# A fused attention and mixture kernel: FFN matmuls in runs of ten at even steps, attention sums in runs of four at odd steps

## The chip, the cores and the metric

One Trainium2 chip, 8 cores, one program on all of them. Each core takes 1024 of the 8192 tokens (half a sequence of 2048) and reads the other half of its sequence for the keys; no core talks to another. The metric is the device time in microseconds of the slowest core. The engines are named as the profile names them: PE (TensorE), PEld (its weight loads), DVE (VectorE), ACT (ScalarE), POOL (GpSimd), SP (SyncE).

## What is computed

```python
xn = layernorm(x)                                   # x: 4 x 2048 x 4096
C_q, C_kv = xn @ Wq_d + bq_d, xn @ Wkv_d + bkv_d    # 12 and 4 columns
q = (C_q @ W_qk + b_qk) as 32 heads of 4
attn = softmax(q @ C_kv.T / 2)                      # per head, 2048 keys
s = (attn @ (C_kv @ Wv_u + bv_u)) @ Wo + bo         # heads of 128
base = xn @ base_W.T                                # 4096 x 4096
top 2 of 28 experts by xn @ gate_W.T, softmax of the two
lora = sum over experts of gate * 2 * (xn @ lora_A.T) @ lora_B.T
x = x + s * silu(base + lora)
```

## The kernel before

The layout is transposed: features on the 128 partitions, the core's T = 1024 tokens along the free axis, in two chunks of 512 (NCH = 2), so nearly every step is a pair of matmuls with 512 columns of tokens each. It runs in three stages.

First, statistics of both halves of the sequence, the normalised input xnT (32 blocks of 128 features, bf16, kept in SBUF), the latents cq_b (12 rows), ckv_b (4 rows x 2048 keys), and the gated LoRA activations hg1 and hg2.

Second, the head loop, `for h in range(H)` with H = 32, in which head h of the attention and output block h of the base and LoRA product (the FFN block) are computed together. It has SKT = 16 steps `kt`, one for each block of 128 keys. The matmuls of a head on PE, 138 in all:

- FFN (L846): 68 matmuls into the PSUM region FC, 64 with xnT against the weight block bw_bf and 4 with hg. `emit_ffn(n)` issues the next n of them. Before, kt 0 to 13 issue five each (four at kt 12 and 13).
- scores (L868): one pair for each kt, 4 rows (the latent dimension) by 128 keys, into one of two PSUM pairs, PB[kt % 2]. ACT reads the pair and writes exp into one of the four slots of pbuf (L971).
- a2 (L706): `a2block(t, h, j)` multiplies the exp of key block j with kaug (8 columns: ones and the latent keys) and accumulates over j in the PSUM region A2C, which is one for all heads. It is issued three steps late: at kt 3 the block 0 of head h, and at kt 0, 1 and 2 of the next head the blocks 13, 14 and 15.
- q of the next head (L878) after the scores of kt 6, bcd (L749, the reciprocal of the softmax sum spread over 128 rows) after those of kt 8, and up (L759, the heads' values) after those of kt 10: a pair each, into the PSUM pair that the next scores, those of kt 7, 9 and 11, are to use.

The waits that matter are these. The first a2 block of head h waits, chunk by chunk, for `("a2s", h-1, c)`: DVE copying the finished sums of head h-1 out of A2C (L904), which itself waits for block 15. The scores of kt wait for exp of kt-2, and those of kt 7, 9 and 11 wait, chunk by chunk, for DVE to have emptied the pair: `("qev", ...)` (L911), `("dcp", ...)` (L770) and `("uptt", ...)` (L776). Exp of kt waits for a2 of kt-4 (pbuf has four slots). `W(eng, *keys)` puts such waits on an engine; each engine works through its list in order. ACT also makes the reciprocal of the sum (L978, L981) behind exp 5. The FFN block of head h is scaled by DVE (L919) into fsb and stored by POOL, and the next FFN block waits for that. The weight block of head h+2 is loaded by POOL when the last FFN matmul of head h is done.

Third, the output projection (L1041), 2048 matmuls, with silu, product and residual on ACT and DVE.

Behind the last head stand a2 blocks 13 to 15, bcd and up of head 31 alone.

Of the kernel before, what the change touches and what calls it, by code (L numbers as in the profile page):

```python
# [20 lines left out]
def build(cfg):  # L21
# [3 lines left out]
    SKT = (2 * T) // 128  # L25
# [46 lines left out]
    with es:  # L72
# [64 lines left out]
        def I(instr, sem, key=None, n=1):  # L137
            cnt[sem] += n
            instr.then_inc(sems[sem], n)
            if key is not None:  # L140
                reg(key, sem)
            return instr
# [6 lines left out]
        def W(eng, *keys):  # L149
            best = {}  # L150
            for k in keys:
                if k is None or k not in EV:
                    continue
                s, v = EV[k]
                if v > 0:
                    best[s] = max(best.get(s, 0), v)
            for s, v in best.items():
                eng.wait_ge(sems[s], v)

        def vself(v):  # L160
            if cnt["sV"] > 0:
                v.wait_ge(sems["sV"], cnt["sV"])
# [532 lines left out]
        def a2block(t, hh, j, explicit_exp=False):  # L695
            if explicit_exp:
                W(t, ("exp", hh, j))
            u = hh * SKT + j
            mm = None
            for c, (c0, cw) in enumerate(CH):  # L700
                if j == 0:
                    if hh > 0:
                        W(t, ("a2s", hh - 1, c))
                    elif c == 0:
                        W(t, ("ckev1",), ("kgo",))
                mm = t.matmul(arena[0:8, A2C + c0:A2C + c0 + cw],  # L706
                              kaug[:, 8 * j:8 * j + 8],
                              pbuf[:, (u % NPB) * T + c0:(u % NPB) * T + c0 + cw],
                              start=(j == 0), stop=(j == SKT - 1),
                              skip_group_check=True)  # L710
            I(mm, "sT", ("a2", hh, j))
# [95 lines left out]
        for h in range(H):  # L807
            base_s = cnt["sS"]
            for kt in range(SKT):
                extra = 2 if (kt > DKT and h > 0) else 0  # L810
                EV[("exp", h, kt)] = ("sS", base_s + kt + 1 + extra)
            base_s += SKT + (2 if h > 0 else 0)
            cnt["sS"] = base_s
            if h == H - 1:
                EV[("dinv", h)] = ("sS", base_s + 2)
            else:
                EV[("dinv", h)] = ("sS", base_s + DKT + 3)
            off = cnt["sV"]
            if h > 0:
                for c in range(NCH):  # L820
                    EV[("a2s", h - 1, c)] = ("sV", off + c + 1)
                off += NCH
            if h + 1 < H:
                for ci in range(NCH):
                    EV[("qev", h + 1, ci)] = ("sV", off + ci + 1)
                off += NCH
            if h > 0:
                for qc in range(NCH):
                    EV[("dcp", h - 1, qc)] = ("sV", off + qc + 1)
                off += NCH  # L830
                for qc in range(NCH):
                    EV[("uptt", h - 1, qc)] = ("sV", off + qc + 1)
                off += NCH
            EV[("fcp", h)] = ("sV", off + 1)

            @block.tensor
            def _(t, h=h):
                fq = list(ffn_mms(h))
                fpos = [0]

                def emit_ffn(n):
                    while n > 0 and fpos[0] < len(fq):
                        lhsT, rhs, c0, cw, st_, sp_ = fq[fpos[0]]
                        if fpos[0] == 0:
                            W(t, ("wLb", h), ("fcp", h - 1))
                        mm = t.matmul(arena[0:128, FC + c0:FC + c0 + cw], lhsT, rhs,  # L846
                                      start=st_, stop=sp_, skip_group_check=True)
                        if fpos[0] == len(fq) - 1:
                            I(mm, "sT", ("fT", h))
                        fpos[0] += 1  # L850
                        n -= 1

                for kt in range(SKT):
                    if kt < SKT - 2:
                        emit_ffn(-(-(len(fq) - fpos[0]) // (SKT - 2 - kt)))
                    if kt < 3:
                        if h > 0:
                            a2block(t, h - 1, SKT - 3 + kt)
                    else:
                        a2block(t, h, kt - 3)  # L860
                    p = kt % 2
                    if kt == 0:
                        W(t, ("qev", h, NCH - 1))
                    spair[(h, kt)] = PB[p]
                    mm = None
                    for c, (c0, cw) in enumerate(CH):
                        W(t, pair_free[p][c])
                        mm = t.matmul(arena[0:128, PB[p] + c0:PB[p] + c0 + cw],  # L868
                                      ckv_b[0:KL, kt * 128:(kt + 1) * 128],
                                      qbs[h % 2][0:KL, c0:c0 + cw],  # L870
                                      start=True, stop=True, skip_group_check=True)
                    I(mm, "sT", ("sc", h, kt))
                    pair_free[p] = [("exp", h, kt)] * NCH
                    if kt == QKT and h + 1 < H:
                        pq = (kt + 1) % 2
                        for ci, (c0, cw) in enumerate(CH):
                            W(t, pair_free[pq][ci])
                            I(t.matmul(arena[0:KL, PB[pq] + c0:PB[pq] + c0 + cw],  # L878
                                       wqk_b[0:QL, (h + 1) * KL:(h + 2) * KL],
                                       cq_b[0:QL, c0:c0 + cw], start=True, stop=True,  # L880
                                       skip_group_check=True), "sT", ("q", h + 1, ci))
                        qloc[h + 1] = PB[pq]
                        pair_free[pq] = [("qev", h + 1, ci) for ci in range(NCH)]
                    if kt == BKT and h > 0:
                        emit_bcd(t, h - 1, (kt + 1) % 2)
                    if kt == UKT and h > 0:
                        emit_up(t, h - 1, (kt + 1) % 2)
                emit_ffn(len(fq))

            if h > 0:  # L890
                @block.gpsimd
                def _(g, h=h):
                    W(g, ("fcp", h - 1))
                    I(g.dma_start(out=dgs.ap()[(h - 1) * 128:h * 128, :], in_=fsb[:, :]),
                      "dF" if (h - 1) % 2 == 0 else "dH", ("fst", h - 1), n=16)

            @block.vector
            def _(v, h=h):
                if h > 0:
                    for c, (c0, cw) in enumerate(CH):  # L900
                        vself(v)
                        W(v, ("a2", h - 1, SKT - 1), ("up", h - 3, NCH - 1),
                          ("dinv", h - 3) if h >= 3 else None)
                        Ip(v.tensor_copy(a2bs[(h - 1) % 2][0:8, c0:c0 + cw],  # L904
                                         arena[0:8, A2C + c0:A2C + c0 + cw]),
                           "sV", ("a2s", h - 1, c))
                if h + 1 < H:
                    for ci, (c0, cw) in enumerate(CH):
                        vself(v)
                        W(v, ("q", h + 1, ci))  # L910
                        inst = v.tensor_scalar(qbs[(h + 1) % 2][0:KL, c0:c0 + cw],  # L911
                                               arena[0:KL, qloc[h + 1] + c0:qloc[h + 1] + c0 + cw],
                                               bqk_f[:, h + 1:h + 2], QSC, ALU.add, ALU.mult)
                        Ip(inst, "sV", ("qev", h + 1, ci))
                if h > 0:
                    emit_vtail(v, h - 1)
                vself(v)
                W(v, ("fT", h), ("fst", h - 1))
                Ip(v.tensor_tensor(fsb[:, :], arena[0:128, FC:FC + T], rs_bf[:, :],  # L919
                                   ALU.mult), "sV", ("fcp", h))  # L920

            if h + 2 < H:
                emit_bwload(h + 2)
# [257 lines left out]
```

## Time and profile before

| what | us |
| --- | --- |
| time before, median of 2 runs | 1897.3 (1895.04 to 1899.57) |
| time of the profiled execution | 1905.4 |
| its span, slowest core (core 2) | 1902.6 |
| spans of the eight cores | 1883.3 to 1902.6 |
| PE busy | 1721.0 (90%) |
| ACT busy | 693.5 (36%) |
| DVE busy | 386.7 (20%) |
| mean granted clock of PE, by core | 0.933 to 0.939 |

The profile is one execution, seen on its slowest core. Busy time of PE includes matmuls that wait in its pipeline: their ends are modelled, and one matmul is shown longer than the distance to the next one's start, so distances between starts are what counts for pace. A timeline row merges like instructions that follow each other: the first number is the start of the first, the second the time to the end of the last, xN their count. The granted clock is 1.0 for 2.4 GHz and 0.5 for 1.2 GHz.

### The profile page before, as it was taken

The numbers are of one execution on the slowest core, as the hardware profiler recorded it, in microseconds if no ns is written. First come the engines' busy times: TensorE is split into PE (matmuls) and PEld (weight loads), VectorE is DVE, ScalarE is ACT, GpSimd is POOL, SyncE is SP. The second block draws the span as 40 slices with busy tenths as digits, with TensorE's granted clock in tenths as the row PEclk, the third lists the DMA queues.
The fourth block names the chain that finished last, engine by engine and source line by source line (L and its number), as shares of the span: only waits on it lengthen the run. The fifth ranks groups of instructions, "written<-read, shape, count | busy, mean of one in ns | idle before, by whom it ended". The sixth has DMA issues, their size and how long they took to land.

```text
span 1902.6 us, 20135 instructions; the slowest of 8 cores (1883.3 to 1902.6 us)
## 1 busy us (share of the span) xinstructions
PE 1721.0 (90%) x7186; PEld 541.7 (28%) x7186; DVE 386.7 (20%) x482; ACT 693.5 (36%) x680; POOL 312.0 (16%) x409
## 2 busy tenths in 40 slices
PE   3569435999999999999999999999995999999997
PEld 0123001222222222222222222222222444444443
DVE  0045231111212112112121121121211111111111
ACT  2310421555555555555555555555550000000000
POOL 4213201010110100101101001011002222222220
PEclk7679555999999999999999999999997999999999
DMA  9959834242242332422423324224207999999997
GB/s 84 127 81 135 134 58 44 28 52 32 28 56 29 37 47 29 54 30 28 56 28 38 46 28 55 29 28 56 28 12 85 170 174 175 169 177 161 181 161 142
DMA packets 318021, 148.08 MB, mean 78 GB/s; under 512 B 290932, under 2 KB 291076, under 8 KB 317700
## 3 DMA queue, kind: packets, MB, share of 16 engines
q0 software_dynamic: 303776, 104.78, 50.2%
q1 hardware_dynamic: 14152, 42.03, 6.2%
q8 instruction: 62, 1.02, 0.2%
q14 instruction: 31, 0.25, 0.1%
HBM read 217.97 MB, written 25.17 MB: 128 GB/s over the span
## 4 chain that ended last, share of the span: by engine, by line
PE 83%; DMA 10%; DVE 3%; ACT 2%; issue 1%; POOL 0%; DVEq 0%; ACTq 0%; POOLq 0%; SPq 0%
PE arena L846 27%; PE arena L1041 23%; PE arena L868 14%; PE arena L706 14%; DMA xst<-xT_own 6%; DMA xst<-xT_oth 3%; DMA wo_bf<-wo 1%; ACT xsq L634 1%; DVE xnT L376 1%; PE arena L878 1%; PE arena L749 1%; PE arena L759 1%; DMA bw_bf<-bwt 1%; PE arena L225 1%; PE arena L231 0%
## 5 line engine op out<-in xcount | busy, mean ns | idle before, releaser
L971 ACT ACTIVATE pbuf<-arena 128x1024 bf16<-128x1024 f32 x512 | 522.9, 1021 | 520.8 <-PE arena L868 517.1
L846 PE MATMUL arena<-xnT,bw_bf 128*128 128x512 bf16 x2048 | 518.5, 384 | 15.6 <-DMA bw_bf<-bwt 15.6
L1041 PE MATMUL arena<-aoT,wo_bf 128*128 128x512 bf16 x2048 | 444.9, 380 | 18.2 <-DMA wo_bf<-wo 18.2
L868 PE MATMUL arena<-qb,ckv_b 4*128 4x512 bf16 x1024 | 309.1, 381 | 0.0
L706 PE MATMUL arena<-pbuf,kaug 128*8 128x512 bf16 x1024 | 306.6, 379 | 0.6 <-ACT pbuf L971 0.3
L1041 PEld LDWEIGHTS arena<-aoT,wo_bf 128*128 128x128 bf16 x2048 | 200.8, 98 | 262.7 <-issue 23.2
L722 POOL DMA_DIRECT2D bw_bf<-bwt x128 | 112.5, 900 | 970.1 <-PE arena L706 927.6
L846 PEld LDWEIGHTS arena<-xnT,bw_bf 128*128 128x128 bf16 x2048 | 166.9, 98 | 338.8 <-issue 196.5
L1055 ACT ACTIVATE g_f<-gsl 128x1024 f32<-128x1024 f16 x32 | 33.8, 1057 | 415.3 <-DVE ost L1069 415.3
L1023 POOL DMA_DIRECT2D wo_bf<-wo x128 | 112.2, 897 | 336.0 <-PE arena L1041 324.4
L634 ACT ACTIVATE xsq<-xst 128x1024 bf16<-128x1024 bf16 x64 | 67.6, 1056 | 176.0 <-DMA xst<-xT_oth 115.4
L868 PEld LDWEIGHTS arena<-qb,ckv_b 4*128 4x128 bf16 x1024 | 56.4, 92 | 219.7 <-issue 219.7
L706 PEld LDWEIGHTS arena<-pbuf,kaug 128*8 128x8 bf16 x1024 | 48.6, 84 | 222.7 <-issue 222.6
L225 PE MATMUL arena<-xst,ones 128*8 128x512 bf16 x128 | 60.1, 568 | 55.3 <-ACT xsq L634 55.3
L911 DVE TENSOR_SCALAR qb<-arena,bqk_f 4x512 bf16<-4x512 f32 x62 | 45.8, 739 | 286.5 <-PE arena L878 281.0
L904 DVE CAST a2b<-arena 8x512 bf16<-8x512 f32 x62 | 42.1, 679 | 260.1 <-PE arena L706 252.8
L1064 DVE SCALAR_TENSOR_TENSOR ost<-arena,bo_f,g_f 128x1024 f32<-128x1024 f32 x32 | 41.1, 1284 | 199.4 <-PE arena L1041 199.4
L1069 DVE TENSOR_TENSOR ost<-ost,g_f 128x1024 f32<-128x1024 f32 x32 | 39.2, 1225 | 187.5 <-DMA g_f<-xT_own 187.5
L770 DVE COPY dinvb<-arena 128x512 f32<-128x512 f32 x64 | 44.3, 692 | 119.8 <-PE arena L749 113.9
L919 DVE TENSOR_TENSOR fsb<-arena,rs_bf 128x1024 f16<-128x1024 f32 x32 | 39.2, 1225 | 135.6 <-PE arena L846 135.6
L776 DVE TENSOR_TENSOR aoT<-arena,dinvb 128x512 bf16<-128x512 f32 x64 | 44.3, 692 | 109.8 <-PE arena L759 103.8
L479 PE MATMUL arena<-xst,wkv_b 128*4 128x512 bf16 x64 | 32.4, 608 | 32.7 <-ACT xsq L634 29.3
(128 smaller groups left out, 601.1 us busy)
## 6 DMA issues: line engine op xcount, KB each, us to landing
bw_bf<-bwt POOLq DMA_DIRECT2D x128, 256.0 KB, 7.9
wo_bf<-wo POOLq DMA_DIRECT2D x128, 256.0 KB, 7.8
xst<-xT_own POOLq DMA_DIRECT2D x64, 256.0 KB, 5.8
g_f<-xT_own SPq DMA_DIRECT2D x32, 512.0 KB, 5.7
outT<-ost SPq DMA_DIRECT2D x32, 512.0 KB, 4.3
xst<-xT_oth POOLq DMA_DIRECT2D x32, 256.0 KB, 5.3
gscr<-fsb POOLq DMA_DIRECT2D x32, 256.0 KB, 8.6
gsl<-gscr SPq DMA_DIRECT2D x32, 256.0 KB, 4.5
```

The lines of the kernel that those rows point to most:

```text
L225: t.matmul(arena[0:8, ca + c0:ca + c0 + cw], ones8[:, :], xst[:, sl * T + c0:sl * T + c0 + cw], start=(kt == 0), stop=(kt == KT - 1), skip ...
L634: Ip(s.activation(xsq[:, (kt % 2) * T:(kt % 2 + 1) * T], xst[:, sl * T:(sl + 1) * T], AF.Square), "sS", (bk, "sq", kt))
L706: mm = t.matmul(arena[0:8, A2C + c0:A2C + c0 + cw], kaug[:, 8 * j:8 * j + 8], pbuf[:, (u % NPB) * T + c0:(u % NPB) * T + c0 + cw], start=( ...
L722: I(g.dma_start(out=bw_bf[:, (mo % 2) * D + k0 * 128:(mo % 2) * D + k1 * 128] .rearrange("p (ki c) -> p ki c", ki=gsz), in_=dbwt.ap()[k0 * ...
L770: Ip(v.tensor_copy(dinvb[:, c0:c0 + cw], arena[0:128, bcdloc[hh] + c0:bcdloc[hh] + c0 + cw]), "sV", ("dcp", hh, qc))
L776: Ip(v.tensor_tensor(aoT[:, hh * T + c0:hh * T + c0 + cw], arena[0:128, uploc[hh] + c0:uploc[hh] + c0 + cw], dinvb[:, c0:c0 + cw], ALU.mul ...
L846: mm = t.matmul(arena[0:128, FC + c0:FC + c0 + cw], lhsT, rhs, start=st_, stop=sp_, skip_group_check=True)
L868: mm = t.matmul(arena[0:128, PB[p] + c0:PB[p] + c0 + cw], ckv_b[0:KL, kt * 128:(kt + 1) * 128], qbs[h % 2][0:KL, c0:c0 + cw], start=True, ...
L911: inst = v.tensor_scalar(qbs[(h + 1) % 2][0:KL, c0:c0 + cw], arena[0:KL, qloc[h + 1] + c0:qloc[h + 1] + c0 + cw], bqk_f[:, h + 1:h + 2], Q ...
L971: inst = s.activation(pbuf[:, sl * T:(sl + 1) * T], arena[0:128, spair[(h, kt)]:spair[(h, kt)] + T], AF.Exp)
L1023: I(g.dma_start(out=wo_bf[:, (mo % 2) * D + k0 * 128:(mo % 2) * D + k1 * 128] .rearrange("p (ki c) -> p ki c", ki=gsz), in_=dwo.ap()[k0 * ...
L1041: mm = t.matmul(arena[0:128, PW + c0:PW + c0 + cw], wo_bf[:, (mo % 2) * D + ki * 128:(mo % 2) * D + (ki + 1) * 128], aoT[:, ki * T + c0:ki ...
```

## The change

Only the order in which a head's matmuls are issued on PE changes. FFN matmuls are issued at the even steps 0 to 12 in seven runs (ten each, the last two nine); a2 blocks are issued at the odd steps, two at a time: at kt = 1 blocks 13 and 14 of head h-1, at kt = 3 block 15 of head h-1 and block 0 of head h, at kt = 5 blocks 1 and 2, and so on to 11 and 12 at kt = 15. Scores, q, bcd and up keep their steps, and so does every wait.

```diff
                 for kt in range(SKT):
-                    if kt < SKT - 2:
-                        emit_ffn(-(-(len(fq) - fpos[0]) // (SKT - 2 - kt)))
-                    if kt < 3:
-                        if h > 0:
-                            a2block(t, h - 1, SKT - 3 + kt)
-                    else:
-                        a2block(t, h, kt - 3)
+                    if kt % 2 == 0 and kt <= SKT - 4:
+                        evens_left = (SKT - 4 - kt) // 2 + 1
+                        emit_ffn(-(-(len(fq) - fpos[0]) // evens_left))
+                    if kt % 2 == 1:
+                        for g_ in (kt - 4, kt - 3):
+                            if g_ < 0:
+                                if h > 0:
+                                    a2block(t, h - 1, SKT + g_)
+                            else:
+                                a2block(t, h, g_)
                     p = kt % 2
```

## Rows read from the trace of the kernel before

**Rows 1.** the page's slices and its chain by line (40 slices of 47.6 us; tenths)

```profile
PE   3569435999999999999999999999995999999997
...
PEclk7679555999999999999999999999997999999999
...
PE arena L846 27%; PE arena L1041 23%; PE arena L868 14%; PE arena L706 14%; DMA xst<-xT_own 6%; DMA xst<-xT_oth 3%; DMA wo_bf<-wo 1%; ACT xsq L634 1%; DVE xnT L376 1%; PE arena L878 1%; PE arena L749 1%; PE arena L759 1%; DMA bw_bf<-bwt 1%
```

**Rows 2.** stretches, PE alone: us, PE busy (count), granted clock, DMA share, GB/s

```profile
313.00:326.00 13.00, 12.98 (x29) 0.50 0.50 49
...
400.00:900.00 500.00, 500.00 (x1999) 1.00 0.33 37
...
1421.80:1425.20 3.40, 1.60 (x7) 1.00 0.16 65
1425.50:1447.50 22.00, 1.86 (x4) 0.50 0.76 81
1447.80:1452.50 4.70, 4.66 (x12) 0.50 1.63 160
1453.00:1470.00 17.00, 17.00 (x80) 1.00 0.23 27
```

**Rows 3.** timeline of PE, kt 2 and 3 of one head: start, us, what

```profile
909.41 0.59 PE L706 MATMUL arena<-pbuf,kaug 128*8 128x512 bf16 x2
909.94 0.60 PE L868 MATMUL arena<-qb,ckv_b 4*128 4x512 bf16 x2
910.47 1.25 PE L846 MATMUL arena<-xnT,bw_bf 128*128 128x512 bf16 x5
911.65 0.65 PE L706 MATMUL arena<-pbuf,kaug 128*8 128x512 bf16 x2
```

**Rows 4.** timeline of PE, behind the last head

```profile
1421.78 1.03 PE L706 MATMUL arena<-pbuf,kaug 128*8 128x512 bf16 x4
1423.11 0.59 PE L706 MATMUL arena<-pbuf,kaug 128*8 128x512 bf16 x2 [0.31 <-ACT pbuf L971]
1428.08 1.01 PE L749 MATMUL arena<-dinv_bf,onesb 1*128 1x512 bf16 x2 [4.38 <-ACT dinv_bf L986]
```

**Rows 5.** timeline of PE, same head, kt 6 and kt 8

```profile
919.49 0.59 PE L878 MATMUL arena<-cq_b,wqk_b 12*4 12x512 bf16 x2
920.02 1.25 PE L846 MATMUL arena<-xnT,bw_bf 128*128 128x512 bf16 x5
...
923.97 0.60 PE L868 MATMUL arena<-qb,ckv_b 4*128 4x512 bf16 x2
924.41 0.59 PE L749 MATMUL arena<-dinv_bf,onesb 1*128 1x512 bf16 x2
```

**Rows 6.** timeline of PE, head 0

```profile
313.01 2.29 PE L846 MATMUL arena<-xnT,bw_bf 128*128 128x512 bf16 x5 [15.61 <-DMA bw_bf<-bwt]
...
324.86 1.01 PE L706 MATMUL arena<-pbuf,kaug 128*8 128x512 bf16 x2
```

**Rows 7.** timeline of DVE, the same head, kt 2 and 3

```profile
910.18 0.68 DVE L904 CAST a2b<-arena 8x512 bf16<-8x512 f32 x1 [8.14 <-PE arena L706]
911.10 0.68 DVE L904 CAST a2b<-arena 8x512 bf16<-8x512 f32 x1 [0.24 <-DVE a2b L904]
```

**Rows 8.** timeline of DVE, the same head, behind q and bcd

```profile
920.89 0.74 DVE L911 TENSOR_SCALAR qb<-arena,bqk_f 4x512 bf16<-4x512 f32 x1 [0.18 <-DVE qb L911]
...
925.76 0.69 DVE L770 COPY dinvb<-arena 128x512 f32<-128x512 f32 x1 [0.17 <-DVE dinvb L770]
```

**Rows 9.** groups by line: busy, mean ns | idle before

```profile
L776 DVE TENSOR_TENSOR aoT<-arena,dinvb 128x512 bf16<-128x512 f32 x64 | 44.3, 692 | 109.8 <-PE arena L759 103.8 <-DVE aoT L776 5.9 <-DVE dinvb L770 0.2
```

**Rows 10.** timeline of ACT, the exp behind the scores of 909.94

```profile
910.63 1.02 ACT L971 ACTIVATE pbuf<-arena 128x1024 bf16<-128x1024 f32 x1 [1.22 <-PE arena L868]
```

**Rows 11.** timeline of PE, end of head 1 and start of head 2

```profile
382.49 0.59 PE L706 MATMUL arena<-pbuf,kaug 128*8 128x512 bf16 x2
...
385.66 1.25 PE L846 MATMUL arena<-xnT,bw_bf 128*128 128x512 bf16 x5
```

## The prediction

> **What bounds the kernel now.** I read the page first: over slices 8 to 30 (the head loop, 313 to about 1421 us) and 31 to 40 TensorE (PE) is busy in nearly every tenth, its granted clock is full, and in the chain that ended last lines 846, 868 and 706 (the three matmul families of the loop) give 27, 14 and 14% of the span [rows 1]. Then the stretches: from 400 to 900 us PE is busy 500.00 of 500.00 us at granted clock 1.00, with 1999 matmuls [rows 2]; a head has 138 (68 FFN, 32 a2, 32 score, 2 each for q, bcd and up), so a head takes 34.5 us, and there is no idle time to win. What a change of order can win is the time that PE loses between matmuls, and what it can lose is a wait that PE does not have today.
>
> Such a loss exists between matmuls of different kinds. A pair of a2 matmuls lasts 0.59 us from start to modelled end, and four in a row 1.03 us [rows 3, 4]; the two more are 0.44, so start to start is 0.22 us inside a run, also across the border from one a2 block to the next with other weights. But a pair of a2 to the following score pair takes 0.53 us, a score pair to the FFN run 0.53, and a run of five FFN matmuls 1.18 [rows 3]. At 0.22 each these would be 0.44, 0.44 and 1.10: every change of kind costs 0.08 to 0.09 us. One change is free: from scores (4 rows x 128 columns) to the bcd pair (1 x 128) it is 0.44; from the q pair (12 x 4) on it is 0.53 again [rows 5]. As a check, 138 x 0.22 + 47 changes (counted below) x 0.09 is 34.6 us.
>
> **What the change saves.** The number of matmuls and their shapes stay. Per head, before: at kt 0 to 13 an FFN run, an a2 pair and a score pair, at kt 14 and 15 an a2 pair and a score pair, and q: 14 x 3 + 4 + 1 = 47 changes of kind (bcd and up are free going in, and share the change that follows). After: each two steps are FFN run of ten, scores, a2 run of four, scores; that is 4 for seven pairs of steps, then score 14 directly behind score 13 (free), a2 run, score 15, and q: 28 + 2 + 1 = 31. Sixteen fewer at 0.09 are 1.44 us a head, 46 us for 32 heads. Head 0 runs at half clock today from 313 to 326 us although PE is fed all the time [rows 2]; the first a2 pair stands at 324.86, and after it the clock rose [rows 6]. The denser FFN runs may lift it some us sooner: I take 2 us, bounds 0 and 5. Saving: 48 us.
>
> **What it loses: four answers of VectorE (DVE).** Each was hidden behind an FFN run of 1.18 us or more; the run moves away.
>
> (1) a2s. The accumulators of head h-1 must be copied by DVE (L904) before a2 of head h may overwrite them. Before, a2 block 15 is at kt 2, a score pair and five FFN matmuls follow, then a2 block 0 at kt 3. In the change both are in the same run at kt 3: a2 block 0 comes directly behind block 15. From the trace: block 15 starts at 909.41, the copies start at 910.18 and 911.10 and last 0.68, so the second ends at 911.78 [rows 3, 7]. Block 0 started at 911.65, and its pair lasts 0.65 rather than 0.59: its second matmul began at 911.65 + 0.65 - 0.37 = 911.93, 0.15 behind the end of the copy (so today this wait is just covered). That is 2.52 us after the start of block 15. In the new order this matmul would be due three spacings after that start, 0.66 us. PE stands 2.52 - 0.66 = 1.86 us, in two parts (the first matmul of block 0 waits for the first copy). Queued behind on PE are score 3 and the FFN run of kt 4; nothing can overtake.
>
> (2) q. The pair goes into the PSUM pair that score 7 needs; DVE moves it out (L911). Q starts at 919.49, the second copy ends at 920.89 + 0.74 = 921.63 [rows 5, 8], with 0.15 of reaction 921.78, or 2.29 after q's start. Cover before: the FFN run, the a2 pair. Cover after: q pair 0.53, a2 run of four 4 x 0.22 + 0.09 = 0.97, first score matmul 0.22: the second is due at 1.72. Loss 0.57 us.
>
> (3) bcd. Starts at 924.41, second copy ends at 925.76 + 0.69 = 926.45 [rows 5, 8], plus 0.15 is 2.19 against 1.72: 0.47 us before the second matmul of score 9.
>
> (4) up. Same form and the same mean duration of the two DVE operations (692 ns, L776) [rows 9]: 0.47 us before score 11.
>
> Sum 3.37 us, in 31 heads (q in heads 0 to 30, the others in 1 to 31): 104 us. Bounds: reaction 0.11 to 0.15 us and spacings 0.216 to 0.22 move each by at most 0.1, the sum by 12 us.
>
> What stays hidden, and by what: exp of score kt starts 0.69 us after the score pair (909.94 to 910.63) and lasts 1.02 [rows 3, 10], so it is usable 1.86 us after the pair's start. The tightest reader is score 14, which needs exp 12: score pair, a2 run and score 13 take 0.53 + 0.97 + 0.44 = 1.94 us. Score 15, which needs exp 13, is due 0.44 + 0.53 + 0.97 = 1.94 behind too, though exp 14 is not needed until the next head. The margin is 0.08 at both; if it were gone it would cost 0.1 a head. Everywhere else an FFN run of ten (2.27 us) lies between, and ScalarE (ACT) has 16 exps of 1.02 and two row operations in 34.5 us. pbuf slots come free as before or earlier. The weight loads on POOL wait for the last FFN matmul, which comes earlier now. In the tail behind the last head the same ACT operations come last.
>
> **What it loses: the clock.** In the loop the clock never fell. The longest stretch without FFN matmuls today is 382.49 to 385.66, 3.2 us, but filled without a gap [rows 11]. Where PE did four a2, a short wait, two more a2, and then waited for DVE and ACT (1421.78 to 1425), the granted clock read 1.00 until 1425.2 and 0.50 from 1425.5 [rows 2, 4]: of a wait of 4.38 us that began at 1423.70 not half had passed. In the new kt 2 and kt 3, between two FFN runs lie scores, two a2 matmuls, a wait, one a2, a wait, one a2, scores: 0.53 + 2.52 + 0.31 + 0.53 = 3.9 us with eight matmuls in it, four of which are 4-row scores. Head 0 also suggests that scores hold up the clock little: from 313.01 to 324.86 FFN runs and scores did not raise it [rows 6]. So I take one fall per head (at some heads none, at others a second one at kt 6 to 11, where stretches of 2.9 to 3.1 us without FFN carry waits of 0.5). Price of one: at 1447.8 PE ran 4.7 us at 0.50 while fully busy before the clock rose [rows 2]; half of that is lost, 2.35 us. In 31 heads 73 us. Bounds: 0 (clock holds) and 6.5 us a head (half of head 0's 13 us).
>
> **Sum.** 104 + 73 - 48 = +129 us. The profiled execution has a span of 1902.6 and took 1905.4 us, giving 2034; it is 8.1 us above the median of 1897.3, so on the median 2026 us.
>
> **Rivals.** A, the forecast: four waits and about one fall of the clock a head, 2026 us.
> B, the waits alone, the clock holds: 1897.3 + 104 - 48 = 1953 us. For it: no single idle gap of PE in the new order exceeds 1.2 us, and the clock was full through today's 3.2 us stretches. Against it: [rows 2, 4], as above.
> The Trainium skill (TensorE: Matmul & The Clock Gate, Why this matters for your kernels) says that drops in the middle of a kernel come from idle gaps between bursts that are clearly longer than any wait here; by that rule B holds and the time is 1953. The fall at 1425 in this trace came before such a gap was over, which is why I put the rule second.
> C, the clock falls at two or more places a head, or stays low as long as in head 0: two falls give 1953 + 146 = 2099, four 2245 us. For it: head 0's 13 us at 0.50. Against it: the new FFN runs of ten last 4.5 us at half clock without a score between, like the stretch at 1447.8 after which the clock rose.
> D, not slower: the three short answers (q, bcd, up) are covered after all and only a2s stalls: 58 - 48 = +10, 1907 us. It decides from the point where q, bcd and up answer 0.5 us sooner than [rows 5, 8] show, and the clock holds as well. Nothing in the rows speaks for that; break-even with all four waits would need a saving of 0.20 us per change of kind where 0.09 is read.
> E, the run of four a2 does not save its change (other weights in each block): 8 x 0.09 x 32 = 23 us less saving, always slower. Against it: the 1.03 us for four [rows 4]. Its chance is in B's and A's ranges.
>
> **How the numbers follow.** A 0.55, B 0.27, C 0.10, D 0.08 (of it 0.02 with a gain over 2%). A measurement of this kernel can tell about 2% from no change, 38 us. A, B and C are slower by more than that: 0.92; same 0.06; faster 0.02. Range: from B less 10 (1943) to about one and a half falls a head, 2070; this leaves out D and C, with the ends 0.2. A's own range is 1990 to 2065.
>
> **What would show it.** In the profile after: FFN runs of ten (2.27 us), a2 runs of four of which the one at kt 3 has two gaps, with releaser DVE L904, of about 1.2 and 0.7 us; scores 7, 9 and 11 with a gap of about 0.5 before their second matmul; idle time before L706 of some 55 us and before L868 of some 45 us; a head period of 34.5 - 1.4 + 3.4 = 36.4 us where the clock holds and 38.8 with one fall; granted clock in 400 to 900 us of about 0.94 instead of 1.00 (1.00 would make B right, below 0.9 C). A period below 35 us would refute the waits; changes of kind that still cost 0.09 inside the a2 run would show E.

## The result

The changed kernel is slower by an eighth: median 2157 us of 11 runs (2139 to 2215) against 1903 us for the kernel before in the same comparison; ratio 1.127, 95% interval 1.124 to 1.130. The ratio, and ratios and times of the experiments, leave out executions in which one die of the chip ran slower than the other or the time was over 1.5% above the fastest, which keeps three of these 11 (2139 to 2148 us) and not the profiled one (2152 us), though its trace shows only the clock levels 1.0 and 0.5. Its runs differ more than those of before because, as will be seen, some cores spend more time at half clock than others, and the slowest core counts. The forecast was 2026 us with a range up to 2070: right in direction, far too small.

The page of the profiled execution (2152 us, span 2150.4, core 4): slices of PE and of its clock, and the three matmul families (busy, mean ns of one | idle before, releaser).

```profile
PE   4587459999999999999999999999999699999998
...
PEclk7687569777779877999997887799777899999999
```

```profile
L846 PE MATMUL arena<-xnT,bw_bf 128*128 128x512 bf16 x2048 | 639.1, 472 | 10.3 <-DMA bw_bf<-bwt 10.3
...
L871 PE MATMUL arena<-qb,ckv_b 4*128 4x512 bf16 x1024 | 342.3, 407 | 34.0 <-DVE qb L914 13.2
L706 PE MATMUL arena<-pbuf,kaug 128*8 128x512 bf16 x1024 | 292.0, 400 | 48.2 <-DVE a2b L907 47.9
```

Against [rows 1], the clock row in slices 8 to 28 is no longer a row of nines but falls to 7. L846, the FFN matmul, did not change, yet its mean went from 384 ns to 472 ns. The row of the kernel before:

```profile
L846 PE MATMUL arena<-xnT,bw_bf 128*128 128x512 bf16 x2048 | 518.5, 384 | 15.6 <-DMA bw_bf<-bwt 15.6
```

And two kinds of idle time are new: 47.9 us before a2, released by the copy of a2s, and 34 us before scores, released by the DVE operations on q, bcd and up.

The cores are far apart: before 1883 to 1903, now

```profile
core 2: 2034.3 us, clock 0.892
...
core 4: 2150.4 us, clock 0.844
```

Core 2's span grew by 132 us against its own of before, core 4's by 257 (before 1893.4). For core 2 this is too kind: its first FFN matmul started at 313.0 us before and at 296.7 us now, and its head loop alone took 153 us longer. The order of work is the same on both cores; the clock is not.

**The waits.** Timeline of core 0, PE and below it DVE, in a head in which the clock stays full: the a2 run of kt 3, and q with the scores of kt 7.

```profile
337.89 0.59 PE L706 MATMUL arena<-pbuf,kaug 128*8 128x512 bf16 x2
339.42 0.38 PE L706 MATMUL arena<-pbuf,kaug 128*8 128x512 bf16 x1 [0.93 <-DVE a2b L907]
340.27 0.38 PE L706 MATMUL arena<-pbuf,kaug 128*8 128x512 bf16 x1 [0.47 <-DVE a2b L907]
...
348.19 0.59 PE L881 MATMUL arena<-cq_b,wqk_b 12*4 12x512 bf16 x2
...
350.48 0.37 PE L871 MATMUL arena<-qb,ckv_b 4*128 4x512 bf16 x1 [0.42 <-DVE qb L914]
...
353.49 0.59 PE L749 MATMUL arena<-dinv_bf,onesb 1*128 1x512 bf16 x2
...
355.67 0.37 PE L871 MATMUL arena<-qb,ckv_b 4*128 4x512 bf16 x1 [0.32 <-DVE dinvb L770]
```

```profile
338.59 0.68 DVE L907 CAST a2b<-arena 8x512 bf16<-8x512 f32 x1 [10.33 <-PE arena L706]
339.44 0.68 DVE L907 CAST a2b<-arena 8x512 bf16<-8x512 f32 x1 [0.17 <-DVE a2b L907]
```

Against [rows 3, 7]: block 15 starts at 337.89, the copies run from 338.59 and 339.44, and the two matmuls of block 0 stand alone with 0.93 and 0.47 us of gap; the second begins 2.38 us behind the start of block 15 (worked out: 2.52; here the second copy followed the first after 0.17 rather than 0.24, and over all heads at full clock the median is 2.51). The second score matmul of kt 7 begins 2.29 us behind q (worked out 2.29), that of kt 9 2.18 us behind bcd (2.19); behind up the median is 2.19 (2.19).

**The clock.** Timeline of the same core and, for the same stretch, the windows of PE (us, PE busy (count), granted clock):

```profile
525.54 0.38 PE L706 MATMUL arena<-pbuf,kaug 128*8 128x512 bf16 x1 [1.00 <-DVE a2b L907]
526.46 0.59 PE L706 MATMUL arena<-pbuf,kaug 128*8 128x512 bf16 x1 [0.54 <-DVE a2b L907]
526.98 1.03 PE L871 MATMUL arena<-qb,ckv_b 4*128 4x512 bf16 x2
527.94 4.45 PE L846 MATMUL arena<-xnT,bw_bf 128*128 128x512 bf16 x10
532.32 1.03 PE L871 MATMUL arena<-qb,ckv_b 4*128 4x512 bf16 x2
...
536.44 3.90 PE L846 MATMUL arena<-xnT,bw_bf 128*128 128x512 bf16 x9 [0.33 <-issue]
```

```profile
330.00:410.00 80.00, 74.44 (x304) 1.00 0.42 49
526.50:539.90 13.40, 13.07 (x30) 0.50 0.00 0
540.20:543.30 3.10, 2.68 (x11) 1.00 0.00 0
543.60:546.80 3.20, 3.20 (x9) 0.50 0.00 0
```

The clock fell at 526.4, between the two matmuls of a2 block 0. From there a pair of scores takes 0.96 us instead of 0.53 and the FFN run of ten 4.38 instead of 2.27, until 540.0; in the next wait, that of score 7 for q, it fell again, for 3.2 us. This head took 44.4 us.

I counted the falls of the granted clock on all cores between 330 and 1280 us in the profiled execution of each kernel, took the distance from one q pair to the next as a head's length, and the time at half clock over heads 2 to 30 of all cores (232 heads). This table is the summary of all runs; experiments follow below.

| kernel | ratio to before (95%) | changes of kind a head | a head without a fall, us | falls, 330 to 1280 us, 8 cores | at half clock, us a head, mean (slowest core) |
| --- | --- | --- | --- | --- | --- |
| before | 1 | 47 | 34.5 | 0 | 0 |
| changed | 1.127 (1.124-1.130) | 31 | 36.6 (few; 18 heads of 232) | 322 | 9.9 (14.5) |
| e1 a2s covered | 1.016 (1.013-1.020) | 32 | 34.5 | 130 | 2.1 (2.5) |
| e2 q, bcd, up covered | 1.015 (1.010-1.019) | 31 | 34.8 | 78 | 1.3 (2.2) |
| e3 all covered | 0.972 (0.969-0.976) | 32 | 33.0 | 0 | 0 |
| e4 before, with the a2s wait | 1.081 (1.074-1.089) | 46 | 36.2 | 140 | 5.9 (6.8) |
| e5a e2 filled, 4 rows | 1.013 (1.010-1.015) | 31 + 2 | 34.8 | 86 | 1.4 (1.4) |
| e5b e2 filled, 128 rows | 1.002 (1.000-1.005) | 31 + 2 | 34.8 | 0 | 0 |
| e6 changed, filled, 128 rows | 1.044 (1.040-1.048) | 31 + 2 | 36.3 | 91 | 1.4 (1.8) |
| e7 e4 filled, 128 rows | 1.034 (1.028-1.039) | 46 + 2 | 36.3 | 0 | 0 |
| v2 score pairs | 0.964 (0.960-0.967) | 27 | 32.5 | 0 | 0 |
| e8 changed, scores 128 rows | 1.007 (1.004-1.010) | 19 | 35.1 | 7 | 0.1 (0.1) |
| e9 before, all 128 | 0.940 (0.936-0.944) | 6 | 30.9 | 0 | 0 |
| v3 v2, all 128 | 0.930 (0.929-0.932) | 6 | 30.5 | 0 | 0 |

### The profile page after: what moved, and what is told of

It is laid out like the page before. It is cut to its first block, busy times and chain, and to the rows that moved or that the text cites. A ratio compares the mean times of both kernels' runs of the same rounds, so it can differ in the third digit from the quotient of the medians.

```text
span 2150.4 us, 20135 instructions; the slowest of 8 cores (2034.3 to 2150.4 us)
## 1 busy us (share of the span) xinstructions
PE 1902.3 (88%) x7186; PEld 627.5 (29%) x7186; DVE 386.6 (18%) x482; ACT 692.2 (32%) x680; POOL 312.0 (15%) x409
## 4 chain that ended last, share of the span: by engine, by line
PE 76%; DVE 11%; DMA 8%; issue 3%; ACT 1%; POOL 1%; DVEq 1%; POOLq 0%; ACTq 0%; SPq 0%
PE arena L846 31%; PE arena L1044 21%; PE arena L871 13%; PE arena L706 8%; DMA xst<-xT_own 4%; DMA xst<-xT_oth 3%; DVE qb L914 2%; DVE aoT L776 2%; DVE dinvb L770 2%; DVE a2b L907 2%; ACT xsq L634 1%; DVE xnT L376 1%; PE arena L225 0%; PE arena L881 0%; PE arena L231 0%
## 5 line engine op out<-in xcount | busy, mean ns | idle before, releaser
L846 PE MATMUL arena<-xnT,bw_bf 128*128 128x512 bf16 x2048 | 639.1, 472 | 10.3 <-DMA bw_bf<-bwt 10.3
L871 PE MATMUL arena<-qb,ckv_b 4*128 4x512 bf16 x1024 | 342.3, 407 | 34.0 <-DVE qb L914 13.2
L706 PE MATMUL arena<-pbuf,kaug 128*8 128x512 bf16 x1024 | 292.0, 400 | 48.2 <-DVE a2b L907 47.9
L846 PEld LDWEIGHTS arena<-xnT,bw_bf 128*128 128x128 bf16 x2048 | 216.0, 114 | 391.3 <-issue 276.3
L871 PEld LDWEIGHTS arena<-qb,ckv_b 4*128 4x128 bf16 x1024 | 66.8, 93 | 305.2 <-issue 303.9
L706 PEld LDWEIGHTS arena<-pbuf,kaug 128*8 128x8 bf16 x1024 | 68.8, 87 | 253.0 <-issue 200.4
L231 PE MATMUL arena<-xsq,ones 128*8 128x512 bf16 x128 | 61.8, 582 | 0.0
```

The costliest lines, as they stand in the source:

```text
L706: mm = t.matmul(arena[0:8, A2C + c0:A2C + c0 + cw], kaug[:, 8 * j:8 * j + 8], pbuf[:, (u % NPB) * T + c0:(u % NPB) * T + c0 + cw], start=( ...
L871: mm = t.matmul(arena[0:128, PB[p] + c0:PB[p] + c0 + cw], ckv_b[0:KL, kt * 128:(kt + 1) * 128], qbs[h % 2][0:KL, c0:c0 + cw], start=True, ...
```

## The experiments

My theory was that each of the four waits costs its time and that the waits, in stretches with little full-size work, make the clock fall. The first rival: the order itself, FFN in lumps, makes it fall, wait or not. The second: it is standing idle alone that counts, not what PE does beside it.

**e1, the a2s wait covered.** Block 15 goes ahead of the FFN run of kt 2.

```diff
+                    if kt == 2 and h > 0:
+                        a2block(t, h - 1, SKT - 1)
                     if kt % 2 == 0 and kt <= SKT - 4:
...
-                                if h > 0:
+                                if h > 0 and g_ < -1:
```

> The changed kernel, but a2 block 15 of the head before is issued at kt 2 ahead of the FFN run, block 0 alone at kt 3, so that the run of ten hides the copy of a2s. Theory (each wait for DVE costs its time, and the waits together with the thin stretch around them make the clock fall): the gaps before L706 go, a head without a fall takes 36.3 - 1.7 + 0.1 = 34.7 us, falls stay only at kt 6 to 11, at most one a head; 1930 to 2010 us. Rival (the order itself, FFN in lumps with long stretches between, makes the clock fall, wait or not): as many falls as in the changed kernel, 2157 - 50 = about 2100 us.

Measured 1932 us, a head without a fall 34.5 us, falls 130 (0.6 a head). The idle time before L706 is gone, that before the scores is as in the changed kernel. As the theory said; the rival is some 170 us off.

```profile
L873 PE MATMUL arena<-qb,ckv_b 4*128 4x512 bf16 x1024 | 318.9, 382 | 34.0 <-DVE qb L916 13.3 <-DVE dinvb L770 10.4 <-DVE aoT L776 10.2
L706 PE MATMUL arena<-pbuf,kaug 128*8 128x512 bf16 x1024 | 269.3, 380 | 0.3 <-ACT pbuf L976 0.3
```

**e2, q, bcd and up covered.** They move one step on, so that an FFN run of the next even step follows.

```diff
-        QKT, BKT, UKT, DKT = 6, 8, 10, 5
+        QKT, BKT, UKT, DKT = 7, 9, 11, 4
```

> The changed kernel, but q, bcd and up go behind the scores of kt 7, 9 and 11 (and the reciprocal behind exp 4), so that the FFN run of the next even step hides DVE's answer; the wait for a2s at kt 3 stays. Theory: three waits of 0.57, 0.47 and 0.47 us go, a head without a fall takes 36.3 - 1.5 = 34.8 us; falls only around kt 3, at two heads in three; 1940 to 2010 us. Rival (order itself): falls stay, about 2110 us.

Measured 1927 us, 13 under the range that was written; 34.8 us a head, falls 78, a third of the heads rather than two thirds. Now it is the other way round: the idle time before the scores is gone, that before L706 stays.

```profile
L871 PE MATMUL arena<-qb,ckv_b 4*128 4x512 bf16 x1024 | 303.1, 380 | 0.0
L706 PE MATMUL arena<-pbuf,kaug 128*8 128x512 bf16 x1024 | 272.9, 379 | 48.3 <-DVE a2b L907 47.9 <-ACT pbuf L974 0.3
```

With all four waits the changed kernel stands some 240 us over before; with either part of them about 30.

**e3, both edits together.**

> Both edits of the two runs before: no wait for DVE is left in the head loop, the runs of ten and the runs of four stay. Theory: the clock stays at full in the loop, a head takes 34.5 - 1.4 + 0.1 = 33.1 to 33.2 us, 1902 - 32 x 1.35 = about 1859 us, ratio 0.977 to the kernel before. Rival (order itself): waits gone, falls stay: about 2050 us.

Measured 1848 us, ratio 0.972: faster than the kernel before. Page groups of it, to compare with those of the changed kernel:

```profile
L873 PE MATMUL arena<-qb,ckv_b 4*128 4x512 bf16 x1024 | 304.4, 382 | 0.0
L706 PE MATMUL arena<-pbuf,kaug 128*8 128x512 bf16 x1024 | 269.3, 380 | 0.3 <-ACT pbuf L976 0.3
```

```profile
330.00:1280.00 950.00, 949.95 (x3968) 1.00 0.36 41
```

No DVE wait, clock 1.00, no fall in 232 heads; the lumps of ten FFN matmuls are all there. The rival (the order itself) has fallen. Of the 11 us under the forecast about 6 are the changes of kind (a head gained 1.55 us where 1.35 was taken), the rest fits head 0, below. Against this kernel, which has the same order and none of the waits, the three short waits of e1 cost 84 us and the a2s wait of e2 79, together 163, but all four together 294.

**e4, the old order with one wait.** Block 15 goes from kt 2 to kt 3 in the kernel before.

```diff
                     if kt < 3:
-                        if h > 0:
+                        if h > 0 and kt < 2:
                             a2block(t, h - 1, SKT - 3 + kt)
                     else:
+                        if kt == 3 and h > 0:
+                            a2block(t, h - 1, SKT - 1)
                         a2block(t, h, kt - 3)
```

> The kernel before with one edit: a2 block 15 of the head before goes from kt 2 to kt 3, directly ahead of block 0, so the wait for a2s appears in the old order with runs of five. It adds 1.7 us of wait and saves two changes of kind (0.2): a head without a fall takes 36.0 us, 1902 + 47 = 1950 us. Theory: the thin stretch of 3.3 us with the wait in it makes the clock fall at some heads: 1960 to 2020 us and a granted clock below 1.00 in the loop. Rival (order itself): clock 1.00 throughout, 1950 us.

Measured 2049 us, ratio 1.081, above even the theory's range. The wait was priced right: moving block 15 saves one change of kind, not the two that were written, and 34.5 + 1.86 - 0.1 is 36.3 us, where 36.2 was measured in a head without a fall. The clock was not. Timeline of PE, core 4, then its stretch:

```profile
737.53 0.38 PE L706 MATMUL arena<-pbuf,kaug 128*8 128x512 bf16 x1 [1.00 <-DVE a2b L906]
738.46 0.38 PE L706 MATMUL arena<-pbuf,kaug 128*8 128x512 bf16 x1 [0.54 <-DVE a2b L906]
...
739.30 1.52 PE L846 MATMUL arena<-xnT,bw_bf 128*128 128x512 bf16 x5
740.74 1.01 PE L706 MATMUL arena<-pbuf,kaug 128*8 128x512 bf16 x2
```

```profile
330.00:1280.00 950.00, 903.35 (x3317) 0.93 0.30 35
```

The gaps are 1.00 and 0.54 us; within the following FFN run (1.52 instead of 1.25) the clock has fallen, and of the 140 falls 88 last 10.2 us. One wait of 1.9 us a head, in the order of runs of five, costs 150 us.

**e5a and e5b, the gaps filled with small and with full matmuls.** Both are e2 with eight extra matmuls between block 15 and block 0 of kt 3, into the PSUM pair that the scores of kt 3 overwrite; nothing else differs between the two.

```diff
                                     a2block(t, h - 1, SKT + g_)
+                                if h > 0 and g_ == -1:
+                                    W(t, *pair_free[1])
+                                    for c0, cw in CH * 4:
+                                        t.matmul(arena[0:128, PB[1] + c0:PB[1] + c0 + cw],
+                                                 <e5a: ckv_b, qbs (4 rows); e5b: bw_bf, xnT (128 rows)>,
+                                                 start=True, stop=True, skip_group_check=True)
```

> The kernel of e2_qbu_odd with the wait at kt 3 filled: between a2 block 15 and block 0 stand eight extra score matmuls (4 rows x 128 columns, those of kt 3 four times over, overwritten by the real ones). PE then has no gap there. If only standing idle makes the clock fall: granted clock 1.00 in the loop, a head takes about 34.8 us, 1910 us. If matmuls with 4 rows hold up the clock little (as head 0 suggested): falls as in e2_qbu_odd although PE is fed, a time like that run's.

> The same with eight extra matmuls of 128 rows x 128 columns (the first FFN operands, into the same PSUM pair) instead of the 4-row ones: same place, same count, same columns. Both readings expect the granted clock 1.00 in the loop and about 34.8 to 35 us a head, 1910 us; if it still falls, the length of the stretch without FFN progress is not what counts and both readings are wrong.

e5a: 1928 us, 86 falls. e5b: 1907 us, none. Timeline of e5a, core 1: PE is fed without a gap, and still the clock falls at 716.3, within the FFN run (which takes 3.92 us, not 2.33).

```profile
711.79 0.60 PE L878 MATMUL arena<-qb,ckv_b 4*128 4x512 bf16 x2
712.33 0.59 PE L706 MATMUL arena<-pbuf,kaug 128*8 128x512 bf16 x2
712.85 1.90 PE L865 MATMUL arena<-qb,ckv_b 4*128 4x512 bf16 x8
714.68 0.59 PE L706 MATMUL arena<-pbuf,kaug 128*8 128x512 bf16 x2
715.21 0.60 PE L878 MATMUL arena<-qb,ckv_b 4*128 4x512 bf16 x2
715.74 3.92 PE L846 MATMUL arena<-xnT,bw_bf 128*128 128x512 bf16 x10
```

The windows of PE in e5a, and below them those in e5b:

```profile
330.00:1280.00 950.00, 949.81 (x3901) 0.98 0.33 38
```

```profile
330.00:1280.00 950.00, 949.82 (x3983) 1.00 0.33 38
```

So standing idle is not needed for a fall: 4-row matmuls in its place do as little for the clock as a gap (86 falls against 78 in e2). The second rival has fallen too.

**e6 and e7, the same filling with full matmuls in the changed kernel and in e4.** (The diff is that of e5b.)

> The changed kernel with q, bcd and up where the change has them (their three waits stay), and the two gaps at kt 3 filled by eight extra matmuls of 128 rows x 128 columns, as in e5b_fill_full. A head without a fall is as long as in the changed kernel, 36.3 us (in e1_a2_15_early it was 34.6). Theory 1 (the falls at kt 3 breed the others: a head lengthened by a fall meets the next waits badly): falls at q, bcd and up as in e1_a2_15_early, 0.6 a head, 1.3 us each; 1897 + 32 x 1.8 + 25 = 1980 us. Theory 2 (what counts is the length of a head, which sets how often the same place of it is met): falls clearly above 0.6 a head, over 2020 us.

> The kernel of e4_before_one_wait (old order, a2 block 15 directly ahead of block 0) with the same filling of 128-row matmuls in its two gaps. The wait's length stays in the head as extra work, the standing idle goes. If the 155 us of e4_before_one_wait were mostly the clock: clock 1.00 in the loop and a head of 36.2 us, 1900 + 31 x 1.7 = 1953 us. If the longer way through the head itself cost them: as e4_before_one_wait, about 2050 us.

e6: 1986 us, a head without a fall 36.3 us, 91 falls, all behind q, bcd and up, and none longer than 3.4 us. This is what theory 1 asked for: with the falls at kt 3 gone the others are even rarer than in e1, although the head is as long as in the changed kernel (but the eight full matmuls also add work to each head, and this run does not keep the two apart). In the changed kernel 69 of the 322 falls lasted 13.7 us and 10 lasted 6.8, and by their place in the head all of these began around the wait of kt 3; the others lasted 3.4. e7: ratio 1.034, clock 1.00, 36.3 us a head. So of e4's 8.1% the wait is about 3.4 and the clock about 4.7.

```profile
330.00:1280.00 950.00, 949.85 (x3819) 1.00 0.35 37
```

**e8, scores in the shape of FFN matmuls.** The changed kernel with all its waits; the 4-row operands are padded with rows of zeros.

```diff
-        ckv_b = sbw(es_mid, "ckv_b", [KL, 2 * T], BF16)
+        ckv_b = sbw(es_mid, "ckv_b", [128, 2 * T], BF16)      # memset 0, rows 0:KL written as before
...
-        qb0 = sbw(es_attn, "qb0", [KL, T], BF16)              # and qb1
+        qb0 = sbw(es_attn, "qb0", [128, T], BF16)             # and qb1; both memset 0
...
-                                      ckv_b[0:KL, kt * 128:(kt + 1) * 128],
-                                      qbs[h % 2][0:KL, c0:c0 + cw],
+                                      ckv_b[:, kt * 128:(kt + 1) * 128],
+                                      qbs[h % 2][:, c0:c0 + cw],
```

> The changed kernel in its own order with all four waits, but both score operands padded with zeros to 128 rows (same columns, same PSUM, 124 rows of zeros), so scores have the shape of FFN matmuls. Theory (4-row matmuls hold the clock up little, and are why the stretches around the waits are thin and why the clock rises so late): far fewer falls, below 0.3 a head instead of 1.5, granted clock 0.98 or more in the loop, though PE stands as long as before. The changes of kind between FFN and scores go as well: 19 left instead of 31, a head without a fall 36.3 - 1.1 = 35.2 us; 1900 + 32 x 0.7 = 1922 us. Rival (the gaps alone decide): falls stay, about 2100 us.

Measured 1918 us; 7 falls instead of 322. Timeline of PE, core 6, kt 3:

```profile
910.40 0.59 PE L707 MATMUL arena<-pbuf,kaug 128*8 128x512 bf16 x2
911.99 0.38 PE L707 MATMUL arena<-pbuf,kaug 128*8 128x512 bf16 x1 [1.00 <-DVE a2b L912]
912.91 0.38 PE L707 MATMUL arena<-pbuf,kaug 128*8 128x512 bf16 x1 [0.54 <-DVE a2b L912]
```

```profile
330.00:1280.00 950.00, 869.77 (x3662) 1.00 0.36 38
```

The gaps of 1.00 and 0.54 us stand where they stood, and the clock holds.

**v2, a further order, and e9 and v3, the padding carried on.** In v2 both score pairs of two steps stand together, a2 of the two steps before behind them, and q, bcd and up behind a2. The edit is against the kernel before, shortened here to what each step does.

```diff
-                for kt in range(SKT): FFN run of five, one a2 block and scores at each kt
+                for kp in range(0, SKT, 2):
+                    emit_ffn(-(-(len(fq) - fpos[0]) // ((SKT - kp) // 2)))
+                    scores of kp and kp + 1
+                    a2block of kp - 2 and kp - 1 (head h - 1 at kp = 0)
+                    q at kp = 6, bcd at 8, up at 10, all into PB[0]; the reciprocal behind exp 3
```

> A further order: for each two steps an FFN run of eight or nine, both score pairs in a row, a2 of the two steps before, and q, bcd and up behind the a2 run of steps 6, 8 and 10, so that the next FFN run hides DVE; the a2s copy is hidden by an FFN run too. 27 changes of kind a head instead of 47 (e3_all_covered has 32). Theory: 34.5 - 20 x 0.09 = 32.7 us a head, clock 1.00 in the loop, 1900 - 32 x 1.85 = about 1838 us. Rival: the second score pair waits for ACT, whose two exps take 2.04 us in a cycle of 3.9 and are late where the reciprocal is made: 0.3 to 0.8 us a head lost, 1850 to 1865 us.

In e9 (the kernel before) and v3 (the kernel of v2) the scores are padded as in e8, and a2 reads 128 columns of kaug from its place instead of 8:

```diff
-                mm = t.matmul(arena[0:8, A2C + c0:A2C + c0 + cw],
-                              kaug[:, 8 * j:8 * j + 8],
+                mm = t.matmul(arena[0:128, A2C + c0:A2C + c0 + cw],
+                              kaug[:, 8 * j:8 * j + 128],
```

> The kernel before in its own order, with the score operands padded to 128 rows of which 124 are zeros, and a2 reading 128 columns of kaug instead of 8 (the extra result rows are not used). Theory (the loss of 0.09 us is paid where the shape changes, whatever the order): 6 changes of kind left of 47, a head 34.5 - 41 x 0.09 = 30.8 us plus about 0.3 of wait for a2s, whose cover shrinks: 31.1; 1900 - 32 x 3.4 = 1790 us. Rival (each matmul with new operands costs it): no gain, 1900 us.

> The order of v2_score_pairs with the padding of e9_before_all_128. Theory: 6 changes left, 138 x 0.2165 + 0.5 = 30.4 us a head, perhaps 0.1 of wait for exp before q; clock 1.00; 1900 - 32 x 4.0 = 1772 us, ratio 0.933. Rival: ACT, with less than 3.6 us for two exps and the reciprocal, becomes late: 1790 us.

Measured 1832 (v2), 1787 (e9) and 1771 us (v3). Timeline of v3, core 6:

```profile
900.41 2.10 PE L851 MATMUL arena<-xnT,bw_bf 128*128 128x512 bf16 x9
902.35 1.03 PE L869 MATMUL arena<-qb,ckv_b 128*128 128x512 bf16 x4
903.22 1.03 PE L707 MATMUL arena<-pbuf,kaug 128*128 128x512 bf16 x4
904.21 0.59 PE L884 MATMUL arena<-cq_b,wqk_b 12*4 12x512 bf16 x2
```

An FFN run of nine takes 1.94 us to the next start, 9 x 0.216: the change to scores is free, as is that from scores to a2 (0.87 for four). Only q still costs its change, and a little more here (0.99 for the a2 run instead of 0.87): it starts at 904.21, 0.14 us behind the end of the exp that frees its PSUM pair (903.04 to 904.07). v3 is the fastest of all, 7.0% under the kernel before.

## Why the prediction failed, by its own steps

**Changes of kind: right.** The saving per change was read as 0.08 to 0.09 us; e3 with 15 fewer gained 1.5 us a head, v2 with 20 fewer 2.0, e9 with 41 fewer 3.6 together with a little new wait. That is 0.10 a change: besides the 0.09, the next matmul in the new kind starts 0.01 us late (0.226 against 0.216). Rival E (the a2 run of four saves nothing) is excluded: such a run takes 0.96 us to the next start in the changed kernel as well.

**The four waits: right.** 3.37 us a head were worked out; e3 to the changed kernel's fall-free heads is 3.3 to 3.6, and each of the four agrees with its median to 0.01 us. Before L706 and the scores the page shows less idle time (48 and 34 us) than the 55 and 45 written, since the modelled end of the matmul before covers a part of each wait. The three short ones are real, so rival D is excluded.

**Exp: right.** No ACT wait of any size appeared in the loop (0.3 us in all before L706).

**Head 0: right sign, too small.** I took 2 us from core 2, where 13 us passed between the first FFN matmul and the rise of the clock. On six of the eight cores it was 21 us and more. In the changed kernel it is 2.9 to 9.3 us on all. Half of the difference, about 7 us, was to be had; it was hidden by the rest. In e3 it shows on seven cores; on core 6, the slowest of its profiled execution, the clock rose only after 25.7 us.

**The clock: the step that failed.** The mechanism was named, its term was mis-sized. The prediction said "I take one fall per head" and "half of that is lost, 2.35 us", 73 us in all. Measured: 1.7 falls a head (322 in 8 x 950 us, 41 us a head) and 9.9 us of half clock a head on the mean, 14.5 on the slowest core, where I had put 4.7. In time, with 1.9 us a head taken off for waits and changes of kind (fall-free heads take 36.3 to 36.6 us against 34.5), the clock cost core 4 257 - 31 x 1.9 = 198 us, 6.4 a head, at the bound of 6.5 that I had written down and then left out of the range. The mean of the eight cores is 4.4 us a head, and core 2, the least touched, lost 153 - 59 = 94 us. So no core came out at the 73 us forecast. Three errors add up:

- the duration of a fall was taken from 1447.8 us [rows 2], where PE does only full-size matmuls. In the head every second run is scores or a2, and [rows 6], cited for this very point just before, shows 12 us of FFN runs and scores at half clock. Spells of 13.7 us occurred.
- rival C was argued down by the FFN run of ten "without a score between". The run is there (527.94, 4.45 us), and the clock rose only 8 us after its end.
- the number was a mean, the metric is the slowest of eight cores: 4.4 us a head on the mean, 6.4 on core 4.

Rival B with its 1953 us is excluded as a description, but its sum is confirmed: e8 and e6 show heads of 35.1 and 36.3 us when the clock holds. The Trainium skill's rule (TensorE: Matmul & The Clock Gate, Why this matters for your kernels), that falls come from idle gaps longer than these, does not hold here: the clock fell with gaps of 1.0 and 0.5 us, and in e5a with none.

**What stays open.** Why all four waits cost more together than e1 and e2 apart. Shown: the long spells begin at kt 3, and heads of one kind follow each other (six of 44.4 us in a row in core 0, seven in core 3, seven of 47.8 us in core 7). Nor are the heads struck at random: in five cores (0, 1, 3, 5, 7) the lengths of the same fourteen heads in a row agree to 0.1 us, short and long ones in the same order. That would fit if the place of a fall depended on the lengths of the heads before, one fall begetting the next; this is argued from these lengths and from e6, not tested by itself.

## What to carry to other kernels

When work is reordered to save fractions of a microsecond, list every wait that the moved work was hiding, and time its answer from the trace against the new distance: that gave four numbers here that were right to 0.01 us. Then ask what the clock will do in the stretch that got thinner, and price it by the slowest core and by the worst spell in the trace, not by the kindest. And before reordering around a change of shape, try to remove it: zero rows and unused columns made scores and a2 the shape of their neighbours and brought 6.0% in the old order, where the best order alone brought 3.6%.

## What the runs showed of the hardware

- A change of shape between matmuls (128 x 128 to 128 x 8, or to 4 x 128) costs 0.09 us and 0.01 more at the next matmul; from 4 x 128 to 1 x 128 or 8 x 128, and between 128 x 128 and 96 x 128, nothing was seen (0.216 us as inside a run). Padding with zeros costs no time: a score matmul of 128 rows goes at 0.22 us like one of 4.
- In these runs the granted clock followed how many rows the matmuls occupy (the 124 added rows hold zeros, so it is not their content), not only whether PE is fed: eight matmuls of 4 rows in a gap, 86 falls; eight of 128 rows in the same gap, none; all scores of 128 rows with the gap open, 7 instead of 322.
- It rose late for the same reason. In head 0 it took 13 to 22 us of continuous work where runs of five alternate with 4-row scores (and, from kt 3 on, 8-column a2 pairs), and 2.9 to 5.3 us in e9, the same order with 128-row scores.
- A wait of 1.9 us in two parts (gaps of 1.00 and 0.54 us in the profile), once in a head of 36 us, cost about 3.4% as a wait and 4.7% as clock (e4, e7).
